# Two layers of pair updates: the right side's sums multiplied into the output weights by ScalarE, and part of the last norm's scale on GpSimd

## The chip, the cores and the metric

The kernel runs on one core of a Trainium2 chip. The metric is the device time of one execution in microseconds; where several runs are given it is their median. One execution of the kernel was also profiled; its span, from the first to the last recorded event, is somewhat shorter than its device time.

## What is computed

The input x is 128 x 128 x 32 (s, r, channel), float32. Two layers follow each other. Cut to what matters:

```python
# layer 0
n = layernorm(x) * ln1_w + ln1_b
left = sigmoid(n @ left1) * (n @ left2);  right = sigmoid(n @ right1) * (n @ right2)
p = layernorm(einsum('nsre,nkre->nske', left, right)) * ln2_w + ln2_b
x1 = x + (p @ out_w) * sigmoid(n @ gate)
# layer 1
left = (x1 @ W_left + b_left) + (x1 @ W_eq + b_eq)
right_sum = sum(x1 @ W_right + b_right, axis=2)      # over r: one vector of 32 per s
o = left * right_sum * sigmoid(x1 @ W_gate + b_gate)
out = layernorm(o @ W_out + b_out + x1) * ln_scale + ln_bias
```

What the change touches is in layer 1: the product with `right_sum`, the product with `W_out`, and the scale of the last norm.

## The kernel before

The work is cut into 8 chunks of 16 values of s (`CHUNKS`, `SPC`), 512 columns each (`COLS`). In the transposed layout a chunk is 128 partitions (4 groups of 32 channels) by 4 blocks (`BLK`) of 128 columns, and each block of columns belongs to four values of s, one for each group of partitions. The sum over r is therefore one number for each partition and block: `rsum[:, c, j]`.

Each engine has its own program, written out by hand, and semaphores join them. Until about 60 us the kernel computes layer 0's norms, the two sides, the einsum on TensorE and its norm's statistics. Then a pipeline runs over i from 0, one chunk further in each iteration, and TensorE, ScalarE, VectorE and GpSimd each have a loop over i with several chunks in flight:

- TensorE (L976): `transpose_t(i)`, `project_q(i-1)` with a transpose of x, in odd iterations `project_sums` (the right side's sums of two chunks at once), `centre_y(i-3)`, `project_1(i-2)` (the gate and the left projection, each as three products of a high and a low part), and last `project_y(i-3)`. `centre_y(c)` and `project_y(c)` add into one bank: x1 with the mean taken off, and oT @ wout.
- ScalarE (L523): `evacuate_tT(i)` (L491), `sums_of_right` in odd iterations (L501), `high1(i-1)` (L497), `gate1(i-2)` (L509), the root of layer 1's variances at i = 5, 7 and 9 (`ROOT3_AT`, L420), `evacuate_y(i-3)` (L516, L517), and after a root one small sigmoid (L547). A root and a sigmoid need different tables, so two table loads go with each of these roots. After the loop come the roots of chunks 6 and 7.
- VectorE (L756): `residual0(i-1)` (L708, L715), which makes x1 and its sums, `scale3` for the chunks in `SCALE_AT`, `variance3(i-4)` (L730), `gated1(i-2)` (L724), which makes `o_a` = left * gate, and `inverse3` (L735). `scale3(c)` multiplies y by the inverse root (L741) and the product by the row `ln_scale` (L744). `SCALE_AT` puts chunks 0 to 3 at i = 6 to 9; chunks 4 and 5 come after the loop. Chunks 6 and 7 don't take `scale3`: TensorE computes them a second time with weights that hold `ln_scale` already (`project_scaled`, L966), and `normalise3` (L751) multiplies by the inverse root straight from the bank. VectorE also adds the bias of chunk 7, in two halves (L788).
- GpSimd (L393): `times_right(c)` (L380) multiplies `o_a` by `rsum` into `oT`, `low1(i-1)` (L372) takes the low part of x1, `normalise2(i+2)` (L364) prepares layer 0's product, and `bias3(c)` (L388) adds the row `ln_bias` to a finished chunk, for chunks 0 to 3 as `BIAS_AT` says, then 4 to 6.
- The SP queue waits for `final`, chunk after chunk, and issues one output transfer of 256 KB for each of chunks 0 to 6 (L259). Chunk 7 leaves as two halves of 128 KB, one by ScalarE's queue (L552) and one by SP's (L262), each after an addition of L788.

Of the kernel before, what the change touches and what calls it, by code (L numbers as in the profile page):

```python
# [59 lines left out]

GATE0_BANK = [0, 1, 3, 4, 5, 6, 7, 3]
GATES_FIRST = 2

# [27 lines left out]
def pair_layers(nc, x, weights, rows, out):  # L93
# [7 lines left out]
    with ExitStack() as ctx:  # L101
# [59 lines left out]
        rsum = sb("rsum", [P, CHUNKS, BLK])  # L161
        sig1 = sb("sig1", [P, 2, COLS])
        o_a = sb("o_a", [P, 2, COLS])
        oT = sb("oT", [P, 2, COLS])

        p_sq = sq[:].rearrange("p s c -> p (s c)").rearrange("p (e s) -> p e s", s=P)

# [9 lines left out]
        def mat(name):  # L177
# [23 lines left out]
        q_ps, xT_ps, x1_ready = sem("q_ps"), sem("xT_ps"), sem("x1_ready")  # L201
        rs_ps, rs_ready, l_ps, g1_ps, sig1_ready = (
            sem("rs_ps"), sem("rs_ready"), sem("l_ps"), sem("g1_ps"), sem("sig1_ready"))
        oa_ready, oT_ready = sem("oa_ready"), sem("oT_ready")
        y_ps, y_ready, ysq_ready = sem("y_ps"), sem("y_ready"), sem("ysq_ready")
        var3, root3, rstd3 = sem("var3"), sem("root3"), sem("rstd3")
        out_scaled, ys_ps = sem("out_scaled"), sem("ys_ps")
        last_half, half_out = sem("last_half"), sem("half_out")
        scaled, final = sem("scaled"), sem("final")


        TT, Q, XT, L, G, RS, Y = 0, 1, 2, 3, 4, 5, 6
# [53 lines left out]
        def _(pool):  # L266
# [105 lines left out]
                nc.gpsimd.tensor_tensor(x1_low[:, c % 2], x1T[:, c % 3], x1_high[:, c % 2],  # L372
                                        ALU.subtract).then_inc(x1_low_ready, 1)

            def times_right(c):
                pool.wait_ge(oa_ready, c + 1)
                pool.wait_ge(rs_ready, c // 2 + 1)
                if c >= 2:
                    pool.wait_ge(y_ps, c - 1)
                nc.gpsimd.tensor_tensor(oT[:, c % 2].rearrange("p (b k) -> p b k", b=BLK),  # L380
                                        o_a[:, c % 2].rearrange("p (b k) -> p b k", b=BLK),
                                        rsum[:, c:c + 1, :].rearrange("p a b -> p b a").to_broadcast([P, BLK, P]),
                                        ALU.mult).then_inc(oT_ready, 1)

            def bias3(c):
                s = slice(c * SPC, (c + 1) * SPC)
                pool.wait_ge(scaled, c + 1)
                nc.gpsimd.tensor_tensor(sq[:, s, :], yn[:, s, :], row_rep[:, 1:2, :].to_broadcast([P, SPC, CH]),  # L388
                                        ALU.add).then_inc(final, 1)

            normalise2(1)

            for i in range(CHUNKS + 2):  # L393
                if i >= 3 and i % 2:
                    times_right(i - 3)
                if 0 <= i - 1 < CHUNKS:
                    low1(i - 1)
                if i >= 3 and i % 2:
                    times_right(i - 2)
                if i + 2 < CHUNKS:  # L400
                    normalise2(i + 2)
                for c in BIAS_AT.get(i, []):
                    bias3(c)
# [4 lines left out]
        def _(act):  # L408
# [90 lines left out]
            def sums_of_right(m):  # L499
# [2 lines left out]
                                     bank[:, RS, 0:2 * BLK], ACT.Identity,  # L502
                                     bias=right_bias[:]).then_inc(rs_ready, 1)

            def gate1(c):
                act.wait_ge(g1_ps, c + 1)
                if c >= 2:
                    act.wait_ge(oa_ready, c - 1)
                nc.scalar.activation(sig1[:, c % 2], bank[:, G], ACT.Sigmoid, bias=gate1_bias[:]  # L509
                                     ).then_inc(sig1_ready, 1)  # L510
# [12 lines left out]
            for i in range(CHUNKS + 3):  # L523
                if i < CHUNKS:
                    evacuate_tT(i)
                if i == 1:
                    act.wait_ge(var2, 2)
                    root(1, FIRST2, P, root2)
                    for c in range(GATES_FIRST, 5):
                        gate0(c)  # L530
                if i == 2:
                    for c in range(5, CHUNKS):
                        gate0(c)
                    act.wait_ge(biases, 3)
                if i >= 3 and i % 2 and i - 2 < CHUNKS:
                    sums_of_right((i - 3) // 2)
                if 0 <= i - 1 < CHUNKS:
                    high1(i - 1)
                if 0 <= i - 2 < CHUNKS:
                    gate1(i - 2)  # L540
                if i in ROOT3_AT:
                    root3_of(ROOT3_AT[i])
                if 0 <= i - 3 < CHUNKS:
                    evacuate_y(i - 3)
                if i in ROOT3_AT and i <= CHUNKS:

                    nc.scalar.activation(scratch[:], eps[:], ACT.Sigmoid)  # L547
# [8 lines left out]
        def _(dve):  # L556
# [162 lines left out]
            def gated1(c):  # L719
                dve.wait_ge(l_ps, c + 1)  # L720
                dve.wait_ge(sig1_ready, c + 1)
                if c >= 2:
                    dve.wait_ge(oT_ready, c - 1)
                nc.vector.scalar_tensor_tensor(out=o_a[:, c % 2], in0=bank[:, L], scalar=leq_bias[:],  # L724
                                               in1=sig1[:, c % 2], op0=ALU.add, op1=ALU.mult).then_inc(oa_ready, 1)

# [10 lines left out]
            def scale3(c):  # L737
                s = slice(c * SPC, (c + 1) * SPC)
                dve.wait_ge(rstd3, holding(ROOTS3, c) + 1)
                dve.wait_ge(y_ready, c + 1)  # L740
                link(nc.vector.tensor_tensor(yn[:, s, :], y[:, s, :],  # L741
                                             rstd[:, 2:3, s].rearrange("p a s -> p s a").to_broadcast([P, SPC, CH]),
                                             ALU.mult))
                nc.vector.tensor_tensor(yn[:, s, :], yn[:, s, :], row_rep[:, 0:1, :].to_broadcast([P, SPC, CH]),  # L744
                                        ALU.mult).then_inc(scaled, 1)

# [37 lines left out]
            for h in (lo, lo + SPC // 2):  # L784
                normalise3(7, h, h + SPC // 2)
            for n, h in enumerate((lo, lo + SPC // 2)):
                dve.wait_ge(scaled, CHUNKS + n)
                nc.vector.tensor_tensor(sq[:, h:h + SPC // 2, :], yn[:, h:h + SPC // 2, :],  # L788
                                        row_rep[:, 1:2, :].to_broadcast([P, SPC // 2, CH]), ALU.add
                                        ).then_inc(last_half, 1)  # L790

        @block.tensor
        def _(pe):
# [162 lines left out]
            def project_y(c):  # L956

                b = Y + c % 2
                pe.wait_ge(oT_ready, c + 1)
                for j in range(BLK):  # L960
                    k = slice(j * P, (j + 1) * P)
                    last = nc.tensor.matmul(in_order(bank[:, b], j), oT[:, c % 2, k], wout_blk[:], start=False,  # L962
                                            stop=j == BLK - 1, skip_group_check=True)
                last.then_inc(y_ps, 1)

            def project_scaled(c):  # L966

                for n, (lhs, rhs) in enumerate(((x1T[:, c % 3], centre_scaled), (oT[:, c % 2], wout_scaled))):
                    for j in range(BLK):
                        k = slice(j * P, (j + 1) * P)  # L970
                        last = nc.tensor.matmul(in_order(bank[:, SCALED + c % 2], j), lhs[:, k], rhs[:],
                                                start=n == 0 and j == 0, stop=n == 1 and j == BLK - 1,
                                                skip_group_check=True)
                last.then_inc(ys_ps, 1)
# [49 lines left out]
```

## Time and profile before

| | |
|---|---|
| Time before, 3 runs | median 115.97 us (115.42 to 117.61) |
| The profiled execution | 116.56 us, its span 114.8 us |
| TensorE, matmuls | busy 88.7 us (77%) |
| TensorE, weight loads (beside the matmuls) | 68.8 us (60%) |
| VectorE | 81.7 us (71%) |
| GpSimd | 69.7 us (61%) |
| ScalarE | 69.6 us (61%) |
| Mean granted TensorE clock | 0.944 |
| Output written | 2.10 MB |

The shares are averages over stages with different limits. An engine counts as busy while it has an instruction in work, also where that instruction itself goes slowly. Times in the rows are microseconds from the start of the span; L with a number is a line of the kernel.

### The profile page before, as it was taken

The page shows a single profiled execution, that of the slowest core. Times are in us where ns is not written, and L with a number is a line of the kernel's source. Part 1 is how long each engine was busy: PE and PEld are TensorE (multiplying, and loading weights), DVE is VectorE, ACT ScalarE, POOL GpSimd, SP SyncE. Part 2 cuts the span into 40 slices and gives each one's busy share as a digit, 9 for nine tenths or more (in the row PEclk, how much of TensorE's full clock was granted, in tenths as well). Part 3 has the DMA queues.
Part 4 walks back from the last instruction along what each step waited for, and adds up shares of the span by engine and source line. Part 5 has one row for each costly group of instructions (what it writes and reads, how often), then busy time and mean ns, then how long its engine had stood idle before and what let it go on. Part 6 is the DMA issues. An engine that isn't in the chain of part 4 may idle for free.

```text
span 114.8 us, 1799 instructions
## 1 busy us (share of the span) xinstructions
PE 88.7 (77%) x566; PEld 68.8 (60%) x566; DVE 81.7 (71%) x239; ACT 69.6 (61%) x121; POOL 69.7 (61%) x83
## 2 busy tenths in 40 slices
PE   1946492499999899996927899999999998795000
PEld 1934271357777699643313587989788796794000
DVE  1528698938888907769997263767798897999910
ACT  0523977846887279981369837466995997841100
POOL 5047963899960009846603978577843869984800
PEclk9999999558999999999999999999999999999955
DMA  4589993000000000000000000000000014539796
GB/s 64 117 139 170 147 146 29 0 0 0 6 0 0 3 6 3 0 0 0 0 0 0 0 6 0 0 3 0 0 0 6 0 17 74 91 51 143 108 145 101
DMA packets 33484, 4.51 MB, mean 39 GB/s; under 512 B 33348, under 2 KB 33476, under 8 KB 33476
## 3 DMA queue, kind: packets, MB, share of 16 engines
q1 hardware_dynamic: 31632, 4.00, 26.8%
q10 hardware_dynamic: 1844, 0.41, 1.9%
q8 instruction: 4, 0.07, 0.3%
q14 instruction: 4, 0.03, 0.1%
HBM read 2.31 MB, written 2.10 MB: 38 GB/s over the span
## 4 chain that ended last, share of the span: by engine, by line
PE 43%; DVE 19%; ACT 10%; POOL 8%; issue 8%; DMA 5%; SPq 2%; DVEq 0%; POOLq 0%
PE bank L820 9%; PE bank L953 6%; POOL acc_q L356 6%; DMA x_tok<-in_x 5%; PE bank L962 5%; PE bank L910 5%; PE bank L805 3%; PE bank L924 3%; PE bank L927 3%; PE bank L925 3%; DVE lr L741 3%; DVE stats L575 3%; DVE lr L590 3%; PE bank L883 2%; ACT gT L480 2%
## 5 line engine op out<-in xcount | busy, mean ns | idle before, releaser
L820 PE MATMUL bank<-lr_blk,xnT 64*128 64x256 f32 x128 | 17.9, 417 | 2.6 <-ACT xnT L431 2.5
L590 DVE TENSOR_TENSOR lr<-bank,sig_lr 128x512 f32<-128x512 f32 x16 | 15.9, 1044 | 4.4 <-ACT sig_lr L441 4.4
L372 POOL TENSOR_TENSOR x_low<-x1T,x_high 128x512 fp32r<-128x512 f32 x8 | 11.1, 1384 | 12.1 <-ACT x_high L497 12.1
L820 PEld LDWEIGHTS bank<-lr_blk,xnT 64*128 64x128 f32 x128 | 12.6, 201 | 6.2 <-issue 2.2
L441 ACT ACTIVATE sig_lr<-bank 128x512 f32<-128x512 f32 x16 | 9.6, 598 | 5.5 <-PE bank L820 5.5
L364 POOL TENSOR_TENSOR t_tok<-p_sb,rstd 128x512 f32<-128x512 f32 x7 | 10.4, 1496 | 2.8 <-DVE rstd L698 2.8
L575 DVE BATCH_NORM_STATS2 stats<-x_tok 128x6 f32<-128x64 f32 x64 | 9.0, 216 | 3.4 <-DMA x_tok<-in_x 3.2
L388 POOL TENSOR_TENSOR sq<-lr,row_rep 128x512 f32<-128x512 f32 x7 | 9.8, 1404 | 2.0 <-DVE lr L744 2.0
L724 DVE SCALAR_TENSOR_TENSOR o_a<-bank,leq_bias,sig 128x512 f32<-128x512 f32 x8 | 6.0, 749 | 6.2 <-ACT sig L509 4.0
L805 PE MATMUL bank<-ident,xc 128*128 128x128 f32 x32 | 6.3, 324 | 5.3 <-POOL xc L292 5.3
L380 POOL TENSOR_TENSOR oT<-o_a,rsum 128x512 f32<-128x512 f32 x8 | 8.7, 1091 | 2.4 <-issue 1.9
L910 PE MATMUL bank<-tT,out_blk 128*128 128x512 f32 x16 | 8.3, 598 | 2.2 <-DVE x1T L715 2.2
L715 DVE SCALAR_TENSOR_TENSOR x1T<-bank,w_rep,u 128x128 f32<-128x128 f32 x32 | 9.3, 348 | 0.3
L962 PEld LDWEIGHTS bank<-wout_blk,oT 128*128 128x128 f32 x64 | 8.2, 191 | 1.9 <-POOL oT L380 1.4
L962 PE MATMUL bank<-wout_blk,oT 128*128 128x128 f32 x64 | 8.5, 276 | 1.0 <-POOL oT L380 1.0
L292 POOL TENSOR_TENSOR xc<-xc,rstd 128x512 f32<-128x512 f32 (+1 forms) x8 | 7.9, 995 | 2.2 <-DVE rstd L582 1.8
L285 POOL TENSOR_TENSOR xc<-x_tok,stats 128x512 f32<-128x512 f32 (+1 forms) x8 | 8.1, 1012 | 1.8 <-DVE stats L575 1.8
L805 PEld LDWEIGHTS bank<-ident,xc 128*128 128x128 f32 x32 | 4.0, 160 | 8.2 <-POOL xc L292 6.3
L953 PE MATMUL bank<-centre_blk,x1T 128*128 128x128 f32 x64 | 8.8, 280 | 0.0
L497 ACT ACTIVATE x_high<-x1T 128x512 fp32r<-128x512 f32 x8 | 5.1, 635 | 5.2 <-DVE x1T L715 5.2
L862 PE MATMUL bank<-lr 128*128 128x128 f32 x64 | 7.4, 277 | 0.5 <-DVE lr L590 0.5
L708 DVE SCALAR_TENSOR_TENSOR u<-bank,q_bias,gT 128x512 f32<-128x512 f32 x8 | 5.9, 736 | 2.7 <-PE bank L910 2.7
(114 smaller groups left out, 216.2 us busy)
## 6 DMA issues: line engine op xcount, KB each, us to landing
x_tok<-in_x SPq DMA_DIRECT2D x14, 128.0 KB, 4.3
out<-sq SPq DMA_DIRECT2D x7, 256.0 KB, 3.3
x_tok<-in_x SPq DMA_DIRECT2D x3, 64.0 KB, 2.5
w_rep<-in_weights ACTq DMA_DIRECT2D x1, 180.5 KB
out<-sq ACTq DMA_DIRECT2D x1, 128.0 KB, 4.6
out<-sq SPq DMA_DIRECT2D x1, 128.0 KB, 4.9
x_tok<-in_x ACTq DMA_DIRECT2D x1, 64.0 KB, 2.8
row_rep<-in_rows ACTq DMA_DIRECT2D x1, 32.0 KB, 5.0
```

The source lines that it names most:

```text
L364: nc.gpsimd.tensor_tensor(place(t_tok[:, c % 2], 0, SPC), even_first(p_sb[:, :, s]), even_first(rstd[:, 1:2, s]).to_broadcast([P, 2, SPC / ...
L372: nc.gpsimd.tensor_tensor(x1_low[:, c % 2], x1T[:, c % 3], x1_high[:, c % 2], ALU.subtract).then_inc(x1_low_ready, 1)
L388: nc.gpsimd.tensor_tensor(sq[:, s, :], yn[:, s, :], row_rep[:, 1:2, :].to_broadcast([P, SPC, CH]), ALU.add).then_inc(final, 1)
L441: nc.scalar.activation(sig_lr[:, j % 3].rearrange("p (s f) -> p s f", f=2 * CH), src[:, :, 0:2 * CH], ACT.Sigmoid).then_inc(lr_sig, 1)
L575: last = nc.vector.bn_stats(stats1[:, k:k + 2, :].rearrange("p s v -> p (s v)"), x_tok[:, k:k + 2, :].rearrange("p s c -> p c s"))
L590: nc.vector.tensor_tensor(lr[:, :, s].rearrange("p f s -> p s f"), src[:, :, 2 * CH:4 * CH], sig_lr[:, j % 3].rearrange("p (s f) -> p s f" ...
L715: nc.vector.scalar_tensor_tensor(out=x1T[:, c % 3, b], in0=bank[:, XT, b], scalar=vec("b_out"), in1=u[:, c % 2, b], op0=ALU.add, op1=ALU.a ...
L805: last = nc.tensor.transpose(bank[:, n % 2, j * P:(j + 1) * P], xc[:, s:s + GRP, :].rearrange("p s c -> p (s c)"), ident[:])
L820: last = nc.tensor.matmul(dst, xnT[half, c, k * P:(k + 1) * P], lr_blk[half].rearrange("p g m c -> p g (m c)"), start=True, stop=True, ski ...
L910: nc.tensor.matmul(bank[:, Q], out0_blk[:], tT[:, c % 2], start=True, stop=True).then_inc(q_ps, 1)
L953: nc.tensor.matmul(in_order(bank[:, b], j), x1T[:, c % 3, k], centre_blk[:], start=j == 0, stop=False, skip_group_check=True)
L962: last = nc.tensor.matmul(in_order(bank[:, b], j), oT[:, c % 2, k], wout_blk[:], start=False, stop=j == BLK - 1, skip_group_check=True)
```

## The change

The sums of the right side go into the weights. (o_a * rsum) @ wout equals o_a @ (rsum * wout), because rsum is one number for each partition in a block. ScalarE makes, for each chunk, four copies of `wout_blk`, each with its rows multiplied by `rsum[:, c, j]` (`right_into_wout`), after `evacuate_tT` and `sums_of_right` and ahead of `high1`. TensorE's `project_y` takes `o_a` and the copy of block j. For chunks 6 and 7 ScalarE makes four more copies, of `wout_scaled`, for `project_scaled` (`right_into_wout_scaled`, after `gate1`). `times_right` and `oT` are gone, and `gated1` waits for `y_ps` where it waited for `oT_ready`.

In the last norm, `scale3` ends after its first multiplication for chunks 0 to 4 (`POOL_SCALES`), and GpSimd does the one by `ln_scale` in `bias3`, ahead of its addition.

```diff
@@ -60,6 +60,7 @@
 
 GATE0_BANK = [0, 1, 3, 4, 5, 6, 7, 3]
 GATES_FIRST = 2
+POOL_SCALES = 5
 
 
 
@@ -161,7 +162,8 @@
         rsum = sb("rsum", [P, CHUNKS, BLK])
         sig1 = sb("sig1", [P, 2, COLS])
         o_a = sb("o_a", [P, 2, COLS])
-        oT = sb("oT", [P, 2, COLS])
+        wout_right = sb("wout_right", [P, 2, BLK, P])
+        wout_right_scaled = sb("wout_right_scaled", [P, 2, BLK, P])
 
         p_sq = sq[:].rearrange("p s c -> p (s c)").rearrange("p (e s) -> p e s", s=P)
 
@@ -201,12 +203,13 @@
         q_ps, xT_ps, x1_ready = sem("q_ps"), sem("xT_ps"), sem("x1_ready")
         rs_ps, rs_ready, l_ps, g1_ps, sig1_ready = (
             sem("rs_ps"), sem("rs_ready"), sem("l_ps"), sem("g1_ps"), sem("sig1_ready"))
-        oa_ready, oT_ready = sem("oa_ready"), sem("oT_ready")
+        oa_ready, wout_right_ready, wout_right_scaled_ready = (
+            sem("oa_ready"), sem("wout_right_ready"), sem("wout_right_scaled_ready"))
         y_ps, y_ready, ysq_ready = sem("y_ps"), sem("y_ready"), sem("ysq_ready")
         var3, root3, rstd3 = sem("var3"), sem("root3"), sem("rstd3")
         out_scaled, ys_ps = sem("out_scaled"), sem("ys_ps")
         last_half, half_out = sem("last_half"), sem("half_out")
-        scaled, final = sem("scaled"), sem("final")
+        normed, scaled, scaled_pool, final = sem("normed"), sem("scaled"), sem("scaled_pool"), sem("final")
 
 
         TT, Q, XT, L, G, RS, Y = 0, 1, 2, 3, 4, 5, 6
@@ -372,31 +375,23 @@
                 nc.gpsimd.tensor_tensor(x1_low[:, c % 2], x1T[:, c % 3], x1_high[:, c % 2],
                                         ALU.subtract).then_inc(x1_low_ready, 1)
 
-            def times_right(c):
-                pool.wait_ge(oa_ready, c + 1)
-                pool.wait_ge(rs_ready, c // 2 + 1)
-                if c >= 2:
-                    pool.wait_ge(y_ps, c - 1)
-                nc.gpsimd.tensor_tensor(oT[:, c % 2].rearrange("p (b k) -> p b k", b=BLK),
-                                        o_a[:, c % 2].rearrange("p (b k) -> p b k", b=BLK),
-                                        rsum[:, c:c + 1, :].rearrange("p a b -> p b a").to_broadcast([P, BLK, P]),
-                                        ALU.mult).then_inc(oT_ready, 1)
-
             def bias3(c):
                 s = slice(c * SPC, (c + 1) * SPC)
-                pool.wait_ge(scaled, c + 1)
+                if c < POOL_SCALES:
+                    pool.wait_ge(normed, c + 1)
+                    nc.gpsimd.tensor_tensor(yn[:, s, :], yn[:, s, :], row_rep[:, 0:1, :].to_broadcast([P, SPC, CH]),
+                                            ALU.mult).then_inc(scaled_pool, 1)
+                    pool.wait_ge(scaled_pool, c + 1)
+                else:
+                    pool.wait_ge(scaled, c + 1 - POOL_SCALES)
                 nc.gpsimd.tensor_tensor(sq[:, s, :], yn[:, s, :], row_rep[:, 1:2, :].to_broadcast([P, SPC, CH]),
                                         ALU.add).then_inc(final, 1)
 
             normalise2(1)
 
             for i in range(CHUNKS + 2):
-                if i >= 3 and i % 2:
-                    times_right(i - 3)
                 if 0 <= i - 1 < CHUNKS:
                     low1(i - 1)
-                if i >= 3 and i % 2:
-                    times_right(i - 2)
                 if i + 2 < CHUNKS:
                     normalise2(i + 2)
                 for c in BIAS_AT.get(i, []):
@@ -502,6 +497,23 @@
                                      bank[:, RS, 0:2 * BLK], ACT.Identity,
                                      bias=right_bias[:]).then_inc(rs_ready, 1)
 
+            def right_into_wout(c):
+
+                act.wait_ge(rs_ready, c // 2 + 1)
+                if c >= 2:
+                    act.wait_ge(y_ps, c - 1)
+                for j in range(BLK):
+                    last = nc.scalar.activation(wout_right[:, c % 2, j], wout_blk[:], ACT.Copy,
+                                                scale=rsum[:, c, j:j + 1])
+                last.then_inc(wout_right_ready, 1)
+
+            def right_into_wout_scaled(c):
+                act.wait_ge(out_scaled, 2)
+                for j in range(BLK):
+                    last = nc.scalar.activation(wout_right_scaled[:, c % 2, j], wout_scaled[:], ACT.Copy,
+                                                scale=rsum[:, c, j:j + 1])
+                last.then_inc(wout_right_scaled_ready, 1)
+
             def gate1(c):
                 act.wait_ge(g1_ps, c + 1)
                 if c >= 2:
@@ -534,10 +546,14 @@
                     act.wait_ge(biases, 3)
                 if i >= 3 and i % 2 and i - 2 < CHUNKS:
                     sums_of_right((i - 3) // 2)
+                if 0 <= i - 3 < CHUNKS:
+                    right_into_wout(i - 3)
                 if 0 <= i - 1 < CHUNKS:
                     high1(i - 1)
                 if 0 <= i - 2 < CHUNKS:
                     gate1(i - 2)
+                if i - 3 >= CHUNKS - 2:
+                    right_into_wout_scaled(i - 3)
                 if i in ROOT3_AT:
                     root3_of(ROOT3_AT[i])
                 if 0 <= i - 3 < CHUNKS:
@@ -720,7 +736,7 @@
                 dve.wait_ge(l_ps, c + 1)
                 dve.wait_ge(sig1_ready, c + 1)
                 if c >= 2:
-                    dve.wait_ge(oT_ready, c - 1)
+                    dve.wait_ge(y_ps, c - 1)
                 nc.vector.scalar_tensor_tensor(out=o_a[:, c % 2], in0=bank[:, L], scalar=leq_bias[:],
                                                in1=sig1[:, c % 2], op0=ALU.add, op1=ALU.mult).then_inc(oa_ready, 1)
 
@@ -738,9 +754,13 @@
                 s = slice(c * SPC, (c + 1) * SPC)
                 dve.wait_ge(rstd3, holding(ROOTS3, c) + 1)
                 dve.wait_ge(y_ready, c + 1)
-                link(nc.vector.tensor_tensor(yn[:, s, :], y[:, s, :],
-                                             rstd[:, 2:3, s].rearrange("p a s -> p s a").to_broadcast([P, SPC, CH]),
-                                             ALU.mult))
+                product = nc.vector.tensor_tensor(yn[:, s, :], y[:, s, :],
+                                                  rstd[:, 2:3, s].rearrange("p a s -> p s a")
+                                                  .to_broadcast([P, SPC, CH]), ALU.mult)
+                if c < POOL_SCALES:
+                    product.then_inc(normed, 1)
+                    return
+                link(product)
                 nc.vector.tensor_tensor(yn[:, s, :], yn[:, s, :], row_rep[:, 0:1, :].to_broadcast([P, SPC, CH]),
                                         ALU.mult).then_inc(scaled, 1)
 
@@ -784,7 +804,7 @@
             for h in (lo, lo + SPC // 2):
                 normalise3(7, h, h + SPC // 2)
             for n, h in enumerate((lo, lo + SPC // 2)):
-                dve.wait_ge(scaled, CHUNKS + n)
+                dve.wait_ge(scaled, CHUNKS + n - POOL_SCALES)
                 nc.vector.tensor_tensor(sq[:, h:h + SPC // 2, :], yn[:, h:h + SPC // 2, :],
                                         row_rep[:, 1:2, :].to_broadcast([P, SPC // 2, CH]), ALU.add
                                         ).then_inc(last_half, 1)
@@ -956,19 +976,22 @@
             def project_y(c):
 
                 b = Y + c % 2
-                pe.wait_ge(oT_ready, c + 1)
+                pe.wait_ge(oa_ready, c + 1)
+                pe.wait_ge(wout_right_ready, c + 1)
                 for j in range(BLK):
                     k = slice(j * P, (j + 1) * P)
-                    last = nc.tensor.matmul(in_order(bank[:, b], j), oT[:, c % 2, k], wout_blk[:], start=False,
+                    last = nc.tensor.matmul(in_order(bank[:, b], j), o_a[:, c % 2, k], wout_right[:, c % 2, j], start=False,
                                             stop=j == BLK - 1, skip_group_check=True)
                 last.then_inc(y_ps, 1)
 
             def project_scaled(c):
 
-                for n, (lhs, rhs) in enumerate(((x1T[:, c % 3], centre_scaled), (oT[:, c % 2], wout_scaled))):
+                pe.wait_ge(wout_right_scaled_ready, c - CHUNKS + 3)
+                for n, lhs in enumerate((x1T[:, c % 3], o_a[:, c % 2])):
                     for j in range(BLK):
                         k = slice(j * P, (j + 1) * P)
-                        last = nc.tensor.matmul(in_order(bank[:, SCALED + c % 2], j), lhs[:, k], rhs[:],
+                        rhs = wout_right_scaled[:, c % 2, j] if n else centre_scaled[:]
+                        last = nc.tensor.matmul(in_order(bank[:, SCALED + c % 2], j), lhs[:, k], rhs,
                                                 start=n == 0 and j == 0, stop=n == 1 and j == BLK - 1,
                                                 skip_group_check=True)
                 last.then_inc(ys_ps, 1)
```

## Rows read from the trace of the kernel before

**Rows 1.** By stretch: length; busy PE, PEld, DVE, ACT, POOL; PEclk, DMA share, GB/s.
```profile
84.00:97.00 13.00, 13.00 (x87) 10.99 (x86) 11.80 (x32) 10.94 (x21) 9.00 (x7) 1.00 0.14 21
97.00:109.50 12.50, 6.78 (x58) 6.33 (x56) 11.88 (x17) 4.67 (x9) 9.77 (x8) 0.97 0.63 96
```

**Rows 2.** Chain of waits, pipeline's end: start, us, what.
```profile
97.02 0.25 PE bank L927
...
98.04 0.70 DVE lr L741
```

**Rows 3.** Timeline of TensorE: start, us, instruction, [idle before, who ended it].
```profile
84.05 1.05 PE L962 MATMUL bank<-wout_blk,oT 128*128 128x128 f32 x8
...
93.68 1.05 PE L962 MATMUL bank<-wout_blk,oT 128*128 128x128 f32 x8
...
98.23 1.16 PE L962 MATMUL bank<-wout_blk,oT 128*128 128x128 f32 x8 [0.97 <-POOL oT L380]
...
103.69 1.06 PE L971 MATMUL bank<-wout_scaled,oT 128*128 128x128 f32 x8
```

**Rows 4.** Timeline of ScalarE.
```profile
78.37 0.63 ACT L497 ACTIVATE x_high<-x1T 128x512 fp32r<-128x512 f32 x1 [1.17 <-DVE x1T L715]
...
83.61 0.58 ACT L491 ACTIVATE tT<-bank 128x512 f32<-128x512 f32 x1
84.09 0.62 ACT L497 ACTIVATE x_high<-x1T 128x512 fp32r<-128x512 f32 x1
...
93.68 0.61 ACT L497 ACTIVATE x_high<-x1T 128x512 fp32r<-128x512 f32 x1
...
97.30 1.28 ACT L420 ACT_TABLE_LOAD   x1
```

**Rows 5.** Groups of ScalarE's instructions by form: busy us, mean ns | idle before.
```profile
L431 ACT ACTIVATE xnT<-bank,w_rep 128x256 f32<-128x256 f32 x2 | 1.1, 556 | 0.3 <-PE bank L805 0.3
...
L420 ACT ACTIVATE std<-st,eps 128x16 f32<-128x16 f32 x2 | 0.6, 308 | 4.3 <-DVE st L730 4.3
...
L547 ACT ACTIVATE scratch<-eps 128x1 f32<-128x1 f32 x2 | 0.4, 204 | 0.0
L420 ACT ACTIVATE std<-st,eps 128x80 f32<-128x80 f32 x1 | 0.4, 361 | 1.8 <-DVE st L688 1.8
```

**Rows 6.** GpSimd: chain of waits, instructions of L380 (min/median/max ns), timeline.
```profile
43.03 1.28 POOL acc_q L356
...
44.45 1.29 POOL acc_q L356
...
L380 POOL TENSOR_TENSOR oT<-o_a,rsum x8: 1040/1042/1429, 67.3 to 98.2; 128x512 f32<-128x512 f32 x8
...
94.37 1.56 POOL L372 TENSOR_TENSOR x_low<-x1T,x_high 128x512 fp32r<-128x512 f32 x1 [1.01 <-ACT x_high L497]
...
106.24 2.56 POOL L388 TENSOR_TENSOR sq<-lr,row_rep 128x512 f32<-128x512 f32 x2 [1.35 <-DVE lr L744]
```

**Rows 7.** VectorE: the instructions of L744 (min/median/max ns), and its timeline.
```profile
L744 DVE TENSOR_TENSOR lr<-lr,row_rep x6: 691/692/1649, 84.1 to 105.5; 128x512 f32<-128x512 f32 x6
...
98.76 1.41 DVE L744 TENSOR_TENSOR lr<-lr,row_rep 128x512 f32<-128x512 f32 x1
```

**Rows 8.** Output transfers: issues of SP's queue, landing, share and rate.
```profile
104.91 0.37 SPq L259 DMA_DIRECT2D out<-sq  x1
...
107.53 0.37 SPq L259 DMA_DIRECT2D out<-sq  x1
...
109.45 1.90 SPq L262 DMA_DIRECT2D out<-sq  x1
...
out<-sq SPq DMA_DIRECT2D x1, 128.0 KB, 4.9
...
110.00:112.00 2.00, 0.00 (x0) 0.00 (x0) 0.00 (x0) 0.00 (x0) 0.00 (x0) 0.50 0.98 149
```

**Rows 9.** Busy time by stretch, first half; PEclk is the granted clock.
```profile
20.00:21.00 1.00, 0.00 (x0) 0.00 (x0) 1.00 (x6) 0.60 (x2) 0.42 (x1) 0.50 0.00 0
```

## Prediction

> **What bounds the kernel now.** I read the profile from its stages. Over 84 to 97 us TensorE is busy for 13.0 of 13.0 us, and over 97 to 109.5 VectorE is, for 11.9 of 12.5 [rows 1]. The chain of waits agrees: it runs on TensorE without a gap to 97.3 and then on VectorE's last norm [rows 2]. So the change meets two bounds: a pipeline in which each iteration is one chunk's TensorE work of about 5 us, and a tail in which VectorE, GpSimd and the output transfers finish the last chunks. The timelines of TensorE, ScalarE and GpSimd [rows 3, 4, 6] then show how late each may be. In the pipeline ScalarE has gaps, but they are not spread evenly: it is idle 1.17 us ahead of `high1` in a plain iteration [rows 4], and has none in iterations 5 to 6 and 7 to 8, where it loads the table for the root and the one for the sigmoid again (1.28 us each). I write y(c) for chunk c's `project_y`.
>
> **What goes.** GpSimd loses eight multiplications by rsum of 1.04 us [rows 6]. In the pipeline that buys nothing: TensorE waited for one only once, 0.97 us ahead of y(6) [rows 3]. VectorE loses five multiplications by the row scale, 0.69 us each where nothing disturbs them, and 1.41 and 1.65 us in the tail [rows 7]. The three in the pipeline are worth nothing while TensorE sets the pace; the two in the tail are 3.1 us of the engine that ends last, if GpSimd and ScalarE keep up. The new wait of o_a on y(c-2) is free: y(c-2) ends an iteration earlier.
>
> **What ScalarE gains.** Four copies of 128x128 with a scale from a pointer, per chunk, and four more for chunks 6 and 7: 40 in all. No such row exists. The nearest is the root over 128x80 with a pointer, from SBUF: 0.361 us; 48 more columns at the 0.83 ns per column between its forms make 0.40 us [rows 5]. Following instructions start 0.1 us before the last ends (0.58 us long, the next 0.48 later [rows 4]), so I take 0.31 us each, and 4 copies = 3 x 0.31 + 0.40 = 1.33 us. From below: the 128x1 without a pointer took 0.204 us; with 127 x 0.83 ns it is 0.31, or 0.21 apart, so 0.95 us for four. From above: 128x256 with two pointers, 0.556 us, 0.46 apart, so 1.94 us.
>
> The Trainium skill (ScalarE: Activation LUTs, "What ACT_TABLE_LOAD costs") gives an ACTIVATE with one pointer operand 186 + 93 + 0.83 per column, an estimate of 386 ns here, 93 of them overlapped: 1.27 us for four against my 1.33, which would lower each stall below by 0.06 us.
>
> The order decides where that lands: `right_into_wout(c)` stands behind `evacuate_tT` and ahead of `high1`. For chunks 0 to 2 the gap ahead of `high1` (1.2 to 1.7 us) covers it to 0.1 us. Chunk 3 isn't covered: `evacuate_tT(6)` starts at 83.61, only because the table load ended then, so the copies run from 84.09 to 85.4, and y(3) was due at 84.05 [rows 3, 4]. **TensorE stalls 1.4 us.** Everything behind it moves by that, the next root and sigmoid load too. In iteration 8 `high1(7)` started at 93.68 straight after a load; that moment becomes 95.2, the copies of chunk 5 stand there until 96.5, and y(5), due at 93.68 + 1.4 = 95.1, **stalls 1.4 us again**. `high1(7)` moves from 93.68 to 96.4, and so does `low1(7)` on GpSimd, from 94.37 to 97.1, ending at 98.4.
>
> From there ScalarE is the queue. Evacuating y(5) to 98.6, sums, copies of chunk 6 to 100.2, `gate1(7)`, the scaled copies to 102.1, table load to 103.3, root, y(6)'s two reads to 104.5, and only then the copies of chunk 7, to 105.9. y(7), which had followed y(6) with nothing but `centre_y(7)` between, starts at 105.9; its two reads end at 108.0, and the roots of chunks 6 and 7 follow at 108.0 and 110.0. TensorE ended at 104.75 [rows 3]; now y(7) and 4 x 0.89 us of scaled products end it at 110.5, and VectorE needs two reads of the bank and two additions of 0.35 to 0.4 us behind that: 112.0 or later, for 109.4.
>
> **What GpSimd gains.** For chunks 0 to 4 a multiplication of the same form as its addition, 1.29 us. The addition waits for the product: where GpSimd feeds itself now, starts are 1.42 us apart (43.03, 44.45), while two independent additions take 2.56 us together [rows 6]. A pair costs 1.42 + 1.25 = 2.67 us. Chunk 0's pair fits between `low1(6)` and `low1(7)`. Chunks 1 to 4 come behind `low1(7)`: 98.4 + 4 x 2.67 = 109.1. VectorE's operations on two SBUF tensors disturb it: GpSimd's multiplication beside one took 1.43 instead of 1.04 us, +0.4 [rows 6], and VectorE's own grew from 0.69 to 1.41 and 1.65 [rows 7]. Four of them are left in this stretch (the rstd product of chunks 3, 4 and 5, the scale of 5): 4 x 0.42 = 1.7. Chunk 4 is ready at 110.8; before, its transfer was issued at 104.91 [rows 8]. Chunks 5 and 6 follow at 112.1 and 113.4. So GpSimd, not VectorE, is last. The bounds: without that disturbance 1.7 less; with a multiplication of 1.04 us, 1.0 less.
>
> The Trainium skill (SBUF — State Buffer, "SBUF: two separate sides") calls the pair of ports that the two engines share an exclusive lock for a whole instruction. Taken as written, each of the four VectorE operations would cost GpSimd its full 0.69, 2.8 us for 1.7, and the sum below would be 1.1 higher; the row shows 0.4.
>
> **The end.** The last transfers form one unbroken stream: over 110 to 112 the queues are 98% busy at 149 GB/s, so 256 KB take 1.8 us. The three at the end (chunk 5 issued at 107.53, chunk 6, two halves) make 3 x 1.8, and the last landed at 109.45 + 4.9 = 114.35 [rows 8]; 107.53 + 5.4 leaves 1.4 us of start. Now four are bunched from chunk 4 on: 110.8 + 1.4 + 4 x 1.8 = 119.4. That is 5.0 us over 114.35. The profiled execution (116.56 us, span 114.8) becomes 121.6 (span 119.8); it lies 0.6 above the median shown, so **121.0**.
>
> **Rivals.**
> A, **longer copies or a fallen clock**: at 1.94 us for four, the two stalls and `low1(7)` move by 2 x 0.6 more: 122.2. Also, TensorE now idles from 102.1 to 105.9 ahead of y(7). After an idle stretch that began at 18.0 its granted clock was 0.50, the 1.2 GHz level, in the window from 20 [rows 9]; after 104.75 it held for about 4 us. If it falls, y(7) and the scaled products cost 4.5 us more, VectorE ends near 116.5, and the last half lands near 120: 121.7.
> B, **GpSimd is little disturbed**: copies at 0.95 us (each stall 0.4 less, `low1(7)` ends at 97.4), no disturbance from VectorE, chunk 4 ready at 97.4 + 10.7 = 108.1, end 116.7: 2.4 over before, 118.3. With some disturbance 119.
> C, the other side, **VectorE's relief decides**: the tail was VectorE's, and 3.1 us leave it; if nothing else is late, 113. It decides only if chunk 4 is ready before 114.35 - 8.6 = 105.7, so `low1(7)` would have to end 5 us before 98.4, earlier than it does now (95.9 [rows 6]). A partial case, in which ScalarE's copies cost TensorE nothing, leaves `low1(7)` at 95.9 and the pairs at 10.7: chunk 4 at 106.6, end 115.2, time 116.9, no change. Against it: no copy fits between 83.61 and 84.05.
>
> **Chances.** Forecast 0.60 (119.3 to 122); A 0.17; B 0.16, of which half within 2%; C 0.07, of which 0.03 faster and 0.04 no change. 2% is about what a measurement of this kernel can tell. Faster 0.03, same 0.12, slower 0.85. The range leaves out C, the lowest part of B and the top of A: 118.0 to 123.4.
>
> **What would show it.** ScalarE: copies of about 0.40 us, 0.31 apart. TensorE: waits of about 1.4 us for ScalarE's copies ahead of y(3) and y(5), none ahead of y(0) to y(2), and one of 3 to 4 us ahead of y(7). GpSimd: busy without a gap from about 97 to 113, pairs of 2.7 us or more, chunk 1's behind `low1(7)`. Chunk 4 issued near 110.8. The prediction is wrong if the copies of chunk 3 end before TensorE is due, if GpSimd has gaps in the tail, or if the last transfers do not queue behind each other.

## The result and the profile after

| | before | changed |
|---|---|---|
| Median | 116.02 us (115.42 to 117.61) | 120.56 us (120.51 to 120.60) |
| Ratio | 1 | 1.040, 95% interval 1.036 to 1.043 |
| Profiled execution, span | 116.56, 114.8 us | 120.58, 118.8 us |

Some executions of a kernel run in a slower state; medians and ranges hold them too, while the ratios are of the faster ones, so that a ratio can be smaller than that of the medians.

The change makes the kernel 4.5 us slower; 5.0 had been forecast. The wait that was forecast is the first thing to look for. The timeline of TensorE in the changed kernel, start, length, instruction, and the idle time before it with what ended it:

```profile
78.64 1.05 PE L983 MATMUL bank<-wout_right,o_a 128*128 128x128 f32 x8
...
85.04 1.13 PE L983 MATMUL bank<-wout_right,o_a 128*128 128x128 f32 x8 [1.31 <-ACT wout_right L506]
...
96.17 1.13 PE L983 MATMUL bank<-wout_right,o_a 128*128 128x128 f32 x8 [1.26 <-ACT wout_right L506]
...
100.03 1.13 PE L983 MATMUL bank<-wout_right,o_a 128*128 128x128 f32 x8 [0.23 <-ACT wout_right L506]
...
105.54 1.13 PE L983 MATMUL bank<-wout_right,o_a 128*128 128x128 f32 x8 [3.48 <-ACT wout_right L506]
```

These are y(2), y(3), y(5), y(6) and y(7). In [rows 3] y(3) and y(5) had no idle time in front, and y(6) waited 0.97 us for GpSimd; y(7) followed without a wait.

The timeline of ScalarE shows why y(3) waits and y(2) does not:

```profile
76.75 1.28 ACT L506 ACTIVATE wout_right<-wout_blk,rsum 128x128 f32<-128x128 f32 x4
77.93 0.61 ACT L492 ACTIVATE x_high<-x1T 128x512 fp32r<-128x512 f32 x1
...
81.75 1.28 ACT L563 ACT_TABLE_LOAD   x1
83.04 0.20 ACT L563 ACTIVATE scratch<-eps 128x1 f32<-128x1 f32 x1
83.15 0.58 ACT L486 ACTIVATE tT<-bank 128x512 f32<-128x512 f32 x1
83.63 1.26 ACT L506 ACTIVATE wout_right<-wout_blk,rsum 128x128 f32<-128x128 f32 x4
```

Chunk 2's copies fill the gap that stood ahead of `high1` in [rows 4] (1.17 us) and end before TensorE wants them. Chunk 3's stand behind a table load and `evacuate_tT`, and TensorE, done with the rest at 83.7, waits until 85.04.

GpSimd's timeline in the tail, and the issues of SP's queue for chunk 4 and for the last half:

```profile
96.62 1.29 POOL L375 TENSOR_TENSOR x_low<-x1T,x_high 128x512 fp32r<-128x512 f32 x1 [2.50 <-ACT x_high L492]
97.85 1.30 POOL L382 TENSOR_TENSOR lr<-lr,row_rep 128x512 f32<-128x512 f32 x1
99.23 1.27 POOL L387 TENSOR_TENSOR sq<-lr,row_rep 128x512 f32<-128x512 f32 x1
100.46 1.27 POOL L382 TENSOR_TENSOR lr<-lr,row_rep 128x512 f32<-128x512 f32 x1
101.81 1.59 POOL L387 TENSOR_TENSOR sq<-lr,row_rep 128x512 f32<-128x512 f32 x1
103.37 1.26 POOL L382 TENSOR_TENSOR lr<-lr,row_rep 128x512 f32<-128x512 f32 x1
104.70 1.60 POOL L387 TENSOR_TENSOR sq<-lr,row_rep 128x512 f32<-128x512 f32 x1
106.26 1.72 POOL L382 TENSOR_TENSOR lr<-lr,row_rep 128x512 f32<-128x512 f32 x1
108.06 4.05 POOL L387 TENSOR_TENSOR sq<-lr,row_rep 128x512 f32<-128x512 f32 x3
...
109.69 0.37 SPq L262 DMA_DIRECT2D out<-sq  x1
...
113.58 2.33 SPq L265 DMA_DIRECT2D out<-sq  x1
```

From `low1(7)` at 96.62 to 112.1 GpSimd has no gap; in [rows 6] it had idled 1.35 us ahead of its last two additions. The transfer of chunk 4 (109.69, for 104.91 in [rows 8]) opens a stream of four times 256 KB (chunks 4 to 6 and the two halves) that lasts to the end: the last half lands 4.8 us after 113.58. The stream by stretch, where the last two numbers are the share and the rate of the transfers:

```profile
111.00:113.00 2.00, 0.86 (x8) 0.67 (x7) 1.03 (x4) 0.00 (x0) 1.11 (x1) 1.00 0.95 144
113.00:115.00 2.00, 0.00 (x0) 0.00 (x0) 0.40 (x2) 0.00 (x0) 0.00 (x0) 1.00 0.94 142
115.00:117.00 2.00, 0.00 (x0) 0.00 (x0) 0.00 (x0) 0.00 (x0) 0.00 (x0) 1.00 0.94 144
```

**A common zero.** The traces differ by up to 2.5 us before the pipeline starts (GpSimd's first `low1` begins between 60.5 and 63.0 us in them), and the medians of the changed kernel's two runs lie 1.3 us apart. So the traces are also compared from the start of GpSimd's first `low1`, 62.08 us in the span before and 61.40 in the changed kernel. From there the end is at 114.8 - 62.08 = 52.7 us before and at 118.8 - 61.40 = 57.4 us after; chunk 4 is issued at 42.8 and at 48.3. The pipeline and the tail alone cost 4.7 us. In the table, all times but the medians are counted so, each from one trace, and the ends hold to 0.1 us:

| kernel | chunk 4 issued | end | median (the same chip's kernel before) |
|---|---|---|---|
| before | 42.8 | 52.7 | 116.0 |
| changed | 48.3 | 57.4 | 120.6 (116.0) |
| changed, again | 48.1 | 57.1 | 121.9 (116.2) |
| fold alone | 45.1 | 55.0 | 119.3 (116.4) |
| scaling alone | 47.9 | 56.2 | 120.0 (116.4) |
| three chunks scaled | 46.5 | 56.4 | 119.5 (116.2) |
| odd copies early | 47.4 | 56.5 | 120.0 (116.4) |
| chunk 7's copies early | 48.5 | 57.5 | 121.2 (116.4) |
| two products more on GpSimd | 50.9 | 59.9 | 123.2 (116.1) |
| fold alone, copies ordered | 44.2 | 54.0 | 117.2 (116.2) |
| fold for chunks 6 and 7 only | 42.0 | 51.8 | 114.7 (116.2) |
| the same, again | 42.1 | 51.9 | 115.7 (116.1) |

### The profile page after: what moved, and what is told of

Same layout as the page of the kernel before. It is cut to its first block, busy times and chain, and to the rows that moved or that the text cites. A ratio compares the mean times of both kernels' runs of the same rounds, so it can differ in the third digit from the quotient of the medians.

```text
span 118.8 us, 1837 instructions
## 1 busy us (share of the span) xinstructions
PE 93.1 (78%) x566; PEld 71.8 (60%) x566; DVE 78.0 (66%) x234; ACT 81.3 (68%) x161; POOL 67.0 (56%) x80
## 4 chain that ended last, share of the span: by engine, by line
PE 36%; ACT 24%; DVE 14%; POOL 8%; issue 6%; DMA 5%; SPq 2%; DVEq 0%; POOLq 0%; ACTq 0%
PE bank L840 9%; POOL acc_q L359 5%; ACT wout_right L506 5%; DMA x_tok<-in_x 5%; PE bank L994 4%; PE bank L983 4%; PE bank L930 4%; ACT L415 3%; PE bank L825 3%; DVE stats L591 3%; DVE lr L606 3%; PE bank L903 2%; ACT L563 2%; POOL xc L288 2%; ACT lr L529 2%
## 5 line engine op out<-in xcount | busy, mean ns | idle before, releaser
L375 POOL TENSOR_TENSOR x_low<-x1T,x_high 128x512 fp32r<-128x512 f32 x8 | 10.3, 1290 | 22.8 <-ACT x_high L492 22.7
L983 PE MATMUL bank<-wout_right,o_a 128*128 128x128 f32 x64 | 8.7, 279 | 6.3 <-ACT wout_right L506 6.3
L983 PEld LDWEIGHTS bank<-wout_right,o_a 128*128 128x128 f32 x64 | 8.1, 191 | 8.0 <-issue 7.7
L930 PE MATMUL bank<-tT,out_blk 128*128 128x512 f32 x16 | 8.9, 640 | 2.2 <-DVE x1T L731 2.2
L506 ACT ACTIVATE wout_right<-wout_blk,rsum 128x128 f32<-128x128 f32 x32 | 10.2, 393 | 0.1
L894 PE MATMUL bank<-xnT,gate_blk 128*128 128x512 f32 x16 | 8.2, 639 | 0.0
```

The source lines that it names most:

```text
L506: last = nc.scalar.activation(wout_right[:, c % 2, j], wout_blk[:], ACT.Copy, scale=rsum[:, c, j:j + 1])
L930: nc.tensor.matmul(bank[:, Q], out0_blk[:], tT[:, c % 2], start=True, stop=True).then_inc(q_ps, 1)
L983: last = nc.tensor.matmul(in_order(bank[:, b], j), o_a[:, c % 2, k], wout_right[:, c % 2, j], start=False, stop=j == BLK - 1, skip_group_c ...
```

## The experiments

### Each part alone

The first kernel takes the second part back:

```diff
-POOL_SCALES = 5
+POOL_SCALES = 0
```

> Undoes the second part: VectorE scales all chunks again, the fold stays. Theory (after the stalls GpSimd's queue is last, because each of chunks 1 to 4 takes 2.7 us or more there): ScalarE and TensorE stay as in the changed kernel (stalls of 1.3 us ahead of y(3) and y(5), 3.5 us ahead of y(7)), GpSimd has only seven additions of 1.25 us and gets gaps, chunk 4 is issued near 107 instead of 109.7, and the end is then set by VectorE and the two halves near 113.5: about 1.5 us less than the changed kernel, 119.0, still 3 over the kernel before. Rival (TensorE and VectorE are last, through y(7)'s wait): no change, 120.5, or more, because VectorE has its five multiplications back.

Ratio to the kernel before 1.014 (1.004 to 1.024), median 119.28 us of executions between 118.27 and 120.86; the profiled one took 118.42. TensorE's waits are those of the changed kernel (1.31, 1.26, 0.22 and 3.49 us), and still chunk 4 leaves 3.2 us earlier and the end comes 2.4 us earlier. GpSimd has gaps again, in its timeline:

```profile
102.85 1.26 POOL L387 TENSOR_TENSOR sq<-lr,row_rep 128x512 f32<-128x512 f32 x1 [2.32 <-DVE lr L764]
105.46 1.27 POOL L387 TENSOR_TENSOR sq<-lr,row_rep 128x512 f32<-128x512 f32 x1 [1.35 <-DVE lr L764]
108.09 1.27 POOL L387 TENSOR_TENSOR sq<-lr,row_rep 128x512 f32<-128x512 f32 x1 [1.35 <-DVE lr L764]
```

These are chunks 3, 4 and 5. The gain is larger than the 1.5 us expected: I had taken VectorE and the halves to be last there, near 113.5, and the last half was issued at 111.95. One thing besides GpSimd differs between the two traces. TensorE's clock fell in the changed kernel behind the wait ahead of y(7), and held here behind the same wait (shown at the end), so its scaled products were done sooner. That this is not what gains the 2.4 us rests on a run below: with chunk 7's copies early the clock held as well, and the end was that of the changed kernel.

The second kernel is the kernel before with only `scale3` and `bias3` changed as in the change:

```diff
+POOL_SCALES = 5
...
+                if c < POOL_SCALES:
+                    product.then_inc(normed, 1)
+                    return
```

> The second part alone on the kernel before: no fold, rsum multiplied into o_a by GpSimd as before, GpSimd scales chunks 0 to 4. Theory: the stalls of 1.3 us ahead of y(3) and y(5) are gone, but GpSimd now has both its old multiplications and the pairs, so y(6) waits for it longer than 0.97 us (about 2.5) and chunk 4 is issued about as late as in the changed kernel (near 110): 119.5 to 121. Rival (the fold's copies on ScalarE are what costs, the scaling on GpSimd is nearly free): 116 to 117.

Ratio 1.029 (1.020 to 1.039), median 119.96 us. TensorE does not wait ahead of y(3) or y(5), but 2.75 us ahead of y(6), for GpSimd:

```profile
98.01 2.94 POOL L381 TENSOR_TENSOR oT<-o_a,rsum 128x512 f32<-128x512 f32 x2
...
99.56 1.16 PE L973 MATMUL bank<-wout_blk,oT 128*128 128x128 f32 x8 [2.75 <-POOL oT L381]
```

Its end (56.2) lies 3.5 us over the kernel before, the fold's 2.3 us, both parts' 4.7. The two do not add up in full. That the fold takes eight multiplications off the queue that the scaling fills is the likely reason, which no run isolates. Against the changed kernel chunk 4 leaves only 0.4 us earlier and the end comes 1.2 us earlier: ScalarE's half was issued at 108.41, ahead of chunk 4 (109.53), so that only three and a half times 256 KB follow chunk 4's issue.

### Is GpSimd's queue the bound?

Two products into a tile that is written again later, ahead of the product of chunk 1 and of chunk 2:

```diff
+                    if c in (1, 2):
+                        nc.gpsimd.tensor_tensor(sq[:, s, :], yn[:, s, :], row_rep[:, 0:1, :].to_broadcast([P, SPC, CH]),
+                                                ALU.mult)
```

> The changed kernel with one more product of 128x512 on GpSimd, of no use, ahead of the product of chunk 1 and of chunk 2. Theory (from the end of low1(7) GpSimd's queue has no slack up to chunk 4, and the output stream follows it): two times 1.25 us come through in full, chunk 4 is issued at 50.7 us from GpSimd's first low1 for 48.2, and the time rises by 2.5 us, to 123 to 124. Rival (TensorE and VectorE are last, through y(7)): GpSimd has slack, 120.5 to 121.5.

Ratio 1.065 (1.059 to 1.072). Chunk 4 is issued 2.6 us later and the end comes 2.5 us later: both products come through in full. Their place has no slack. TensorE's wait ahead of y(7), 3.48 us, and its clock, which fell behind it, are as in the changed kernel's trace, so the end moved with GpSimd's queue alone.

Three chunks scaled for five:

```diff
-POOL_SCALES = 5
+POOL_SCALES = 3
```

> The changed kernel with three chunks scaled by GpSimd for five. Theory (GpSimd's queue up to chunk 4, then the output stream): two products of about 1.4 us leave the queue ahead of chunk 4, which is issued 2.8 us sooner (45.5 us from GpSimd's first low1), as without any scaling there; the end falls by 2 to 2.5 us like in the run without the second part, since the pairs of chunks 1 and 2 run while GpSimd would wait for VectorE anyway: 118 to 118.5. Rival (each pair costs its share, also the early ones): 1 us less than the changed kernel, 119.5.

Against the changed kernel on the same chip the median falls from 121.88 to 119.51 us (ratios to the kernel before 1.046 and 1.024, the latter from 1.013 to 1.034), a fall as large as forecast. In the trace, which is of the longest of its four executions (121.15 us; the others took 118.65 to 119.65), it is less: chunk 4 is issued 1.6 to 1.8 us earlier, not 2.8, and the end comes 0.7 to 1.0 us earlier. From chunk 3 on GpSimd waits for VectorE, whose two multiplications now stand ahead of each addition:

```profile
105.58 1.26 POOL L387 TENSOR_TENSOR sq<-lr,row_rep 128x512 f32<-128x512 f32 x1 [0.63 <-DVE lr L764]
108.19 1.27 POOL L387 TENSOR_TENSOR sq<-lr,row_rep 128x512 f32<-128x512 f32 x1 [1.36 <-DVE lr L764]
```

So neither expectation holds in whole: the early pairs cost something too, about 1.4 us of chunk 4's time against the fold alone (46.5 and 45.1).

### Does TensorE's wait ahead of y(7) matter?

Chunk 7's copies directly behind chunk 6's, ahead of the root's table load:

```diff
-                if 0 <= i - 3 < CHUNKS:
+                if 0 <= i - 3 < CHUNKS - 1:
                     right_into_wout(i - 3)
+                if i - 3 == CHUNKS - 2:
+                    right_into_wout(CHUNKS - 1)
```

> The changed kernel with only chunk 7's copies moved, to directly behind chunk 6's, ahead of the root's table load. Theory (GpSimd's queue and the output stream are last, not TensorE's idle time): the wait ahead of y(7) falls from 3.5 us to about 1, TensorE's clock stays up in the tail, TensorE and VectorE end some 3 us sooner, and the time falls by 0.5 us at most, 120.1 to 120.6. Rival (TensorE's wait and the lower clock set the end): 2 to 3 us less, 118.

The wait ahead of y(7) falls from 3.48 to 0.47 us, and the granted clock holds, and nothing is gained: ratio 1.037 (1.030 to 1.045) for 1.040 and 1.046 of the two runs of the changed kernel, end 57.5 us for 57.4 and 57.1. TensorE is done 3.4 us sooner, but VectorE only 0.7, not 3: its last two additions took 1.86 us together, for 0.75. The edit has a small cost too, as the root now stands behind four more copies and GpSimd waits 0.63 us for VectorE ahead of chunk 3; chunk 4 is issued 0.2 us later. TensorE's largest wait in the pipeline is off the path that sets the end. The second run of the changed kernel says the same: its clock was low for longer, its last half was issued at 53.1 for 52.2, and its end came no later (57.1).

### Place or amount of the copies?

The odd chunks' copies an iteration early, as soon as their sums are there:

```diff
-                if 0 <= i - 3 < CHUNKS:
+                if i >= 3 and i % 2 and i - 3 < CHUNKS:
                     right_into_wout(i - 3)
...
                     gate1(i - 2)
+                if i >= 3 and i % 2 and i - 2 < CHUNKS:
+                    right_into_wout(i - 2)
```

> The changed kernel with one edit: the copies of the odd chunks (3, 5, 7) are made an iteration earlier, behind the sigmoid of the gate and ahead of the root's table load, where the sums are there already. Theory (place, not amount): no wait of TensorE ahead of y(3) and y(5), the one ahead of y(7) under 1 us, the granted clock stays at the upper level in the tail; but the table loads still move by 1.2 us, so high1(7) starts at about 94.9 for 95.9 and GpSimd's queue behind it ends 1.1 us sooner: 119.4. Rival (stalls of TensorE as such set the end): all 1.3 + 1.3 + 3.5 us come back, 116 or less. Rival (the amount of ScalarE's work decides, not its place): 120.5.

Ratio 1.018 (1.008 to 1.028), all executions 118.66 to 121.17 us; the trace is of the one of 121.17. The waits ahead of y(3), y(5) and y(7) are gone, 6 us in all; TensorE now waits 0.43 us for `evacuate_tT`, 0.54 ahead of y(6) and 1.65 for the scaled copies of chunk 6. At the end 0.9 us are gained, and chunk 4 is issued 0.9 us earlier: `low1(7)` stands behind the same copies and table loads on ScalarE, whether TensorE waits or not. The rest of the time is GpSimd's queue. Both rivals fall. In the trace the size agrees with the 1.1 us worked out; the ratios (1.018 for 1.040 and 1.046) speak for 2.5 us or more, with an interval of 1.2 us to each side, so the size stays open.

Then the same order without the scaling, with the scaled copies behind both evacuations, and with TensorE waiting for them only ahead of the second half of its scaled products:

```diff
-POOL_SCALES = 5
+POOL_SCALES = 0
...
             for b in range(len(ROOT3_AT), len(ROOTS3)):
+                right_into_wout_scaled(CHUNKS - 2 + b - len(ROOT3_AT))
                 root3_of(b)
...
-                pe.wait_ge(wout_right_scaled_ready, c - CHUNKS + 3)
                 for n, lhs in enumerate((x1T[:, c % 3], o_a[:, c % 2])):
+                    if n:
+                        pe.wait_ge(wout_right_scaled_ready, c - CHUNKS + 3)
```

> The fold with its copies in better places and nothing scaled by GpSimd: odd chunks' copies an iteration early ahead of the root's table load, the scaled copies of chunks 6 and 7 behind both chunks' evacuation, and TensorE waits for them only ahead of the second half of its scaled products. Theory (place of the copies costs about 1 us in the pipeline, GpSimd's scaling the rest): 1.5 to 2 us less than the fold alone, about 117, still not under the kernel before, because each table load moves by 1.2 us. Rival (the amount of work on ScalarE decides): 119, like the fold alone.

117.23 us, ratio 1.007 (1.002 to 1.013) for the fold's 1.014, and the end at 54.0 for 55.0: about half of the fold's cost was where the copies stand and what waits for them. What is left, 1.3 us at the end, fits the 1.2 us by which each table load still moves. That this is its cause is argued, not shown.

### A version that beats both

Fold only where GpSimd is short of time and ScalarE is not, chunks 6 and 7; on the kernel before:

```diff
+FOLD_FROM = 6
...
-                if i >= 3 and i % 2:
+                if i >= 3 and i % 2 and i - 3 < FOLD_FROM:
                     times_right(i - 3)
...
+                if i - 3 == FOLD_FROM:
+                    right_into_wout(i - 3)
...
+                if i - 3 == FOLD_FROM:
+                    right_into_wout(i - 2)
```

> The kernel before with the fold for chunks 6 and 7 only: GpSimd multiplies rsum into o_a for chunks 0 to 5 in the pipeline as before, ScalarE makes copies only behind its last gap (16 in all, in the order of the run before). Theory (in the tail GpSimd and VectorE disturb each other, in the pipeline ScalarE must not be burdened): the wait of 0.97 us ahead of y(6) falls to about 0.3, GpSimd loses 2.5 us of work in the tail, VectorE's scales of chunks 3 and 4 take 0.7 instead of 1.4 to 1.65 us, chunk 5 is issued 1.5 to 2 us sooner: 114.5 to 115, under the kernel before. Rival (the copies delay the root's table load and with it the inverse roots as much as they free): 116.

114.65 us, ratio 0.983 (0.971 to 0.994). With five rounds:

> The fold for chunks 6 and 7 only, once more with five rounds: 1.5 to 2% under the kernel before, interval wholly below 1. Rival (the first result was a lucky set of executions): within 1%.

115.65 us, ratio 0.991 (0.986 to 0.996). The sign holds, as both intervals lie below 1. The size does not: at 0.9% it is what the rival gave and not the 1.5 to 2% expected, and it is less than the 2% that the prediction took for the limit of such a measurement. The traces agree with 0.8 to 0.9 us (51.8 and 51.9 for 52.7). In the first run's timeline of VectorE, and in its instructions of the row scale (min/median/max ns):

```profile
98.88 0.69 DVE L767 TENSOR_TENSOR lr<-lr,row_rep 128x512 f32<-128x512 f32 x1
...
L767 DVE TENSOR_TENSOR lr<-lr,row_rep x6: 691/692/693, 83.6 to 104.1; 128x512 f32<-128x512 f32 x6
```

All six multiplications take 0.69 us, where [rows 7] had one of 1.41 and a longest of 1.65. On TensorE, y(6) waits 0.22 us for 0.97, and the new wait for the scaled copies (2.57 us) costs nothing, as VectorE isn't ready for their product:

```profile
96.98 1.13 PE L990 MATMUL bank<-wout_right,o_a 128*128 128x128 f32 x8 [0.22 <-ACT wout_right L512]
...
103.36 1.16 PE L1002 MATMUL bank<-wout_right_scaled,o_a 128*128 128x128 f32 x8 [2.57 <-ACT wout_right_scaled L519]
```

VectorE gains less than its multiplications do: the root that they wait for comes behind eight copies, and VectorE idles 0.67 us ahead of the inverse root.

## Why the prediction was right, point by point

Times of the forecast are put on the common zero here, by taking 62.08 from them.

- **Price of the copies**: 0.40 us forecast, 0.31 apart, 1.33 for four; measured 0.393, and 1.26 to 1.28 for four. The group of ScalarE's instructions:

```profile
L506 ACT ACTIVATE wout_right<-wout_blk,rsum 128x128 f32<-128x128 f32 x32 | 10.2, 393 | 0.1
```

  The estimate from the Trainium skill (ScalarE: Activation LUTs, "What ACT_TABLE_LOAD costs"), 386 ns and 1.27 us for four, was as near for one and the nearer for four.
- **Where they show**: covered for chunks 0 to 2, waits of 1.4 us ahead of y(3) and y(5). Measured none, 1.31 and 1.26.
- **ScalarE as the queue from there**: `low1(7)` ends at 36.3 forecast, (96.62 + 1.29) - 61.40 = 36.5 measured; y(7) starts at 43.8 forecast, 44.1 measured.
- **GpSimd's pairs**: forecast 4 x 2.67 and 1.7 of disturbance, 12.4 us. Measured from 97.91 to 109.69, 11.8. About half of the 0.6 us is the disturbance, which was taken too large: four of GpSimd's instructions took 1.59, 1.60, 1.72 and 1.60 us for 1.27, 1.4 us together. The rest is the undisturbed pair, 2.61 us (starts at 97.85 and 100.46) for 2.67. VectorE's four operations on two SBUF tensors in its timeline:

```profile
101.22 1.07 DVE L757 TENSOR_TENSOR lr<-lr,rstd 128x512 f32<-128x512 f32 x1
...
103.68 1.49 DVE L757 TENSOR_TENSOR lr<-lr,rstd 128x512 f32<-128x512 f32 x1
...
105.70 1.16 DVE L757 TENSOR_TENSOR lr<-lr,rstd 128x512 f32<-128x512 f32 x1
106.89 1.65 DVE L764 TENSOR_TENSOR lr<-lr,row_rep 128x512 f32<-128x512 f32 x1
```

  Each began while a GpSimd instruction was in work and ended 0.54 to 0.56 us after that one (101.73, 104.63, 106.30 and 107.98), whenever it had begun. The GpSimd instruction that started meanwhile took 0.32 to 0.45 us longer; VectorE's operation reached 0.47 to 0.60 us into it. So, by these rows, the two took turns. That agrees with the exclusive lock of the Trainium skill (SBUF — State Buffer, "SBUF: two separate sides"). The 2.8 us that the prediction worked out from it did not come: GpSimd lost only part of what was left of VectorE's operation, never the whole 0.69 us.
- **The stream of transfers**: 109.69 + 1.4 + 4 x 1.8 = 118.3; the last half landed at 113.58 + 4.8 = 118.4.
- **VectorE's end**, 49.9 or later: it was (112.65 + 0.75) - 61.40 = 52.0. The forecast path kept the upper clock; the clock fell, as the second half of rival A had it. It didn't cost what A said, because the stream was already later: with the clock held, in the run with chunk 7's copies early, the end was the same. Chance had a part here: the forecast left the fall out, and it was right without it only because VectorE was not on the path.
- **Rival C** (VectorE's relief decides) is not what happened: VectorE is busy 78.0 us for 81.7, and it waited for the gates, the roots and TensorE. **Rival B** had the direction of its assumptions right, little else: the copies took 1.27 us for four and not 0.95, and the disturbance was 0.8 of my value, not nil. (B's `low1(7)` at 97.4 is mis-added, too: 98.4 less two times 0.4 is 97.6.)

The sum came to 5.0 us. The trace from the common zero has 4.7, the medians 4.5. On the common zero the forecast had chunk 4 issued at 48.7, and it was at 48.3: GpSimd's four pairs took 0.6 us less, and `low1(7)` ended 0.2 us later, although both stalls were 0.1 us shorter than forecast. That last is not explained.

## What to carry to other kernels

Work moved to an engine with idle time is hidden only in the gap where it stands: look up, chunk by chunk, what is behind it (here a table load) and who is due. The sum of the parts on each queue decides in the tail, and there the engine with 56% of busy time was the bound, while TensorE's longest wait in the pipeline (3.5 us) was worth nothing. Where an algebraic change relieves one engine and burdens another, apply it only to the chunks for which that trade is good.

## What the runs showed of the hardware that I had not expected

TensorE's clock can fall after the work has come back, and the same wait need not bring it down. In the first trace of the changed kernel TensorE idled from 102.1 to 105.5, then worked without a gap, and the busy time by stretch (PEclk is the third number from the end) shows the lower level from 107:

```profile
106.00:107.00 1.00, 1.00 (x10) 1.00 (x10) 0.97 (x2) 0.86 (x3) 1.00 (x2) 0.94 0.18 27
107.00:108.00 1.00, 1.00 (x6) 1.00 (x6) 1.00 (x1) 0.98 (x3) 0.98 (x1) 0.50 0.68 105
```

0.50 is the 1.2 GHz level. The 32 scaled products, forecast at 3.6 us, took 5.2. With waits of 0.47 and 1.14 us in the same place, in the run with chunk 7's copies early, the clock stayed at 1.00 to the end of TensorE's work.

Two other traces with a wait of 3.48 and 3.49 us in that place went otherwise. In the second run of the changed kernel the clock fell during the wait, which ended at 106.02. With the fold alone, where the wait ended at 105.69, it stayed at 1.00:

```profile
105.00:106.00 1.00, 0.00 (x0) 0.01 (x1) 1.00 (x2) 1.00 (x5) 0.92 (x2) 0.66 0.98 149
```

```profile
105.69 1.13 PE L983 MATMUL bank<-wout_right,o_a 128*128 128x128 f32 x8 [3.49 <-ACT wout_right L506]
...
107.00:108.00 1.00, 1.00 (x12) 1.00 (x11) 0.96 (x2) 1.00 (x3) 0.00 (x0) 1.00 0.27 42
108.00:109.00 1.00, 1.00 (x12) 1.00 (x11) 0.85 (x4) 0.14 (x2) 0.91 (x1) 1.00 0.96 145
```

Whether such a wait costs clock cannot be read from its length in these runs, and what decides it is not shown.
